# Attention on one core: a head's finishing moved from units 12 to 26 to units 21 to 38 of the next head, projections and latent maxima spread wider

## The reference, cut to what matters

```python
a1 = _attn(q, k1, v1, causal=True)    # keys from a latent
a2 = _attn(q, ks, vs, causal=False)   # 64 selected tokens
a3 = _attn(q, kw, vw, causal=True)    # the "window" keys
out = g[:, 0] * a1 + g[:, 1] * a2 + g[:, 2] * a3
```

## Time and profile before

| | |
|---|---|
| median of three runs | 2782.44 us (2770.95 to 2783.22) |
| the profiled execution | 2779.87 us, its span 2778.1 us |
| PE busy | 2352.7 us, 85% |
| DVE, ACT, POOL busy | 1788.2, 1745.4, 1639.8 us |
| the attention's heads | from 387 us to 2364 us of the span |

### The profile page before, as it was taken

How to read it: one execution, slowest core, us unless ns; L and a number is a source line. 1 busy time by engine, 2 the same in 40 slices (tenths; PEclk the granted TensorE clock), 3 DMA queues, 4 the chain that set the end, 5 groups by cost and what they waited for, 6 DMA issues and landing times. The chain is left out here.

```text
span 2778.1 us, 38402 instructions
## 1 busy us (share of the span) xinstructions
PE 2352.7 (85%) x12402; PEld 1868.3 (67%) x12402; DVE 1788.2 (64%) x2824; ACT 1745.4 (63%) x3574; POOL 1639.8 (59%) x1430
## 2 busy tenths in 40 slices
PE   0278569999999899999999999999999998448885
PEld 0155347777777677777767777777777776448885
DVE  2566357686776768687776868676675763455553
ACT  3433226777777676777767676777777777106663
POOL 5154316767576666767666666766656566006885
PEclk9975559999999999999999999999999999658998
DMA  9757543325051534424151533222132110615776
GB/s 383 320 186 243 167 129 103 86 71 138 20 157 26 132 64 109 97 61 134 40 141 26 138 65 102 56 69 64 24 67 54 31 29 10 186 57 183 193 207 167
DMA packets 199860, 314.87 MB, mean 113 GB/s; under 512 B 95915, under 2 KB 130219, under 8 KB 186731
## 3 DMA queue, kind: packets, MB, share of 16 engines
q1 hardware_dynamic: 189947, 298.23, 37.6%
q0 software_dynamic: 9712, 14.18, 2.7%
HBM read 210.20 MB, written 101.75 MB: 112 GB/s over the span
## 5 line engine op out<-in xcount | busy, mean ns | idle before, releaser
L1391 POOL TENSOR_TENSOR p_lo<-prob,p_hi 128x512 fp32r<-128x512 f32 (+2 forms) x960 | 1096.3, 1151 | 648.0 <-ACT p_hi L1469 513.4
L1467 ACT ACTIVATE prob<-ps_s 128x512 f32<-128x512 f32 (+4 forms) x1344 | 723.3, 538 | 501.0 <-PE ps_s L1484 377.2
L1602 DVE TENSOR_REDUCE max_part<-ps_x 128x1 f32<-128x128 f32 (+1 forms) x1240 | 720.0, 605 | 214.6 <-PE ps_x L1513 131.9
L1469 ACT ACTIVATE p_hi<-ps_s 128x512 fp32r<-128x512 f32 (+3 forms) x1344 | 718.8, 535 | 1.6
L1391 DVE TENSOR_TENSOR p_lo<-prob,p_hi 128x512 fp32r<-128x512 f32 (+1 forms) x320 | 290.3, 907 | 142.3 <-ACT p_hi L1469 133.9
L1570 PE MATMUL ps_o<-p_hi,v_win 128*128 128x512 f32 (+3 forms) x640 | 255.4, 399 | 0.0
L1570 PE MATMUL ps_o<-p_hi,v_lat 128*128 128x512 f32 (+3 forms) x640 | 246.7, 386 | 0.0
L1572 PE MATMUL ps_o<-p_lo,v_win 128*128 128x512 f32 (+3 forms) x640 | 238.5, 373 | 0.0
L1572 PE MATMUL ps_o<-p_lo,v_lat 128*128 128x512 f32 (+3 forms) x640 | 234.5, 367 | 0.0
L1663 DVE TENSOR_TENSOR raw_o<-ps_o,low_sum 32x512 f32<-32x512 f32 x192 | 131.4, 684 | 72.9 <-ACT low_sum L1455 61.4
L1513 PE MATMUL ps_x<-k_hi,head_first 96*128 96x512 f32 (+2 forms) x320 | 123.5, 388 | 42.0 <-DVE max_part L1602 25.5
(11 more groups left out here) (432 smaller groups left out, 5864.5 us busy)
## 6 DMA issues: line engine op xcount, KB each, us to landing
raw<-in_experts_w_dram SPq DMA_DIRECT2D x23, 1536.0 KB
wbuf<-in_tok_weight_dram SPq DMA_DIRECT2D x16, 2000.0 KB, 16.9
head_first<-kw_scratch SPq DMA_DIRECT2D x72, 256.0 KB, 5.0
kw_scratch<-st_hi SPq DMA_DIRECT2D x48, 256.0 KB, 2.9
kw_scratch<-st_lo SPq DMA_DIRECT2D x48, 256.0 KB, 4.4
q_scratch<-st_hi SPq DMA_DIRECT2D x48, 256.0 KB, 3.7
q_scratch<-st_lo SPq DMA_DIRECT2D x48, 256.0 KB, 5.0
head_first<-q_scratch SPq DMA_DIRECT2D x48, 256.0 KB, 6.2
```

The lines of the kernel that those rows point to most:

```text
L1391: ns.tensor_tensor(upper if low else p_lo[:, i % LSLOTS, c:CH], prob[low:P, i % NPROB, c:CH], upper.bitcast(F32), ALU.subtract).then_inc(s ...
L1467: nc.scalar.activation(prob[low:P, i % NPROB, c:CH], ps_s[i % 3][low:P, c:CH], ACT.Exp, scale=SCALE).then_inc(s["p_full"], 1)
L1469: nc.scalar.activation(p_hi[:, i % SLOTS, c:CH], ps_s[i % 3][:, c:CH], ACT.Exp, scale=SCALE).then_inc(s["p_up"], 1)
L1602: ins = nc.vector.tensor_reduce(mpart[:, q, c:c + 1], bank[:, 0:w], axis=AX.X, op=ALU.max)
```

## The change

Three tables move, and three lines of SP's order. No instruction is added or removed.

```diff
         if h + 4 < H:
-            spread(h, prep_tasks(h // 4 + 1, h % 4), *((1, 19) if h else (6, 24)))
-        spread(h, max_tasks(h, LATENT, range(NJ)), 9, HU - 5)
-        spread(h, [("neg", h, 0)], HU - 5, HU - 4)
+            spread(h, prep_tasks(h // 4 + 1, h % 4), *((1, 25) if h else (6, 30)))
+        spread(h, max_tasks(h, LATENT, range(NJ)), 5 if h else 7, HU - 4)
+        spread(h, [("neg", h, 0)], HU - 4, HU - 3)
         if h + 1 < H:
-            spread(h, max_tasks(h + 1, SELECT, None) + max_tasks(h + 1, WINDOW, range(NJ)), HU - 4, NU - 7)
+            spread(h, max_tasks(h + 1, SELECT, None) + max_tasks(h + 1, WINDOW, range(NJ)), HU - 3, NU - 7)
...
-                if h:
-                    store_inverse(h - 1)
-                    load_weight(h - 1)
                 if prep:
                     store_out(gr, j, "kw", 0)
...
                         load_q(h + 1)
                         load_kw(h + 1, 0)
                 if h:
+                    store_inverse(h - 1)
+                    load_weight(h - 1)
                     store_output(h - 1)
...
-        FINISH = {12: 0, 18: 1, 20: 2, 22: 3, 24: 4, 26: 5}
+        FINISH = {21: 0, 30: 1, 32: 2, 34: 3, 36: 4, 38: 5}
```

## The result

| | before | after |
|---|---|---|
| median | 2781.41 us (4 runs, 2770.95 to 2783.22) | 2897.89 us (4 runs, 2888.86 to 2905.29) |
| profiled execution | 2779.87 us | 2888.86 us, span 2887.1 us |

The change is slower: ratio 1.0419, 95% interval 1.0389 to 1.0448, 116 us by the medians. The forecast was +68 and its range ended at +116: the sign was right, the size was not. The median lies 2 us above the range.

The account below looks back on a forecast made before the run. PE, busy for 85% of the span, was taken as the bound, its stalls as what can be won. Terms 16 + 63 - 9 - 2 = +68 us on 2779.9 gave 2848 us, range 2770 to 2896.

Parts of the forecast that it names:

- the eight heads: Heads 1, 2, 4, 5, 6, 8, 9, 10: 127.2 us each, +16 us together, -11 to +44 with all the ends.
- heads 12 to 14: Heads without projections, SP free, weights ahead of step 1: 115.25 us each, -9 us together (-12 to -6).
- head 0: First head, no finishing but six more units for its projections: -2 us (-4 to 0).
- Three heads with loads between: Heads 3, 7 and 11: inverses' store queued behind nine loads, PE stalls 20.2 us, 143.0 us a head: +63 us.
- Chain to the weights: From PE's start of unit 21 through POOL, stores, inverses and weight loads: weights land after 22.9 us, in the eight heads.
- PE stalls for 5.3 us: At unit 33 in the eight heads, PE runs out of `ps_x` banks as DVE awaits weights: 5.3 us, ends 3.5 and 7.2.
- The low clock behind it: Half clock behind the unit 33 stall in the eight heads: 2.5 us a head, between 1.7 and 3.4.
- I leave 1.75 us of stalls per head: Short PE stalls remaining at units 21, 26, 27 and among steps at units 30 to 38: 1.75 us, ends 1.0 and 2.5.
- No wait at step 1: Rival: weights arrive before PE runs out of banks in all eleven heads with projections: 2714 us, chance 0.08.
- Inverses that overtake the loads: Rival: in heads 3, 7 and 11 inverses land before the nine loads, +39 us there: 2814 us, chance 0.10.
- Only three heads wait: Rival: POOL does `st_lo` of kw earlier, so only heads 3, 7 and 11 stall, 15 us: 2770 us, chance 0.08.
- Spreading that does nothing for short stalls: Rival: 1.75 us becomes some 3.5 in 14 heads, +25 us, 2873 us; part of the forecast's chance of 0.74.

Follow-up runs that it names:

- one half: Kernel before with the change's wider tables for projections, maxima and turn; finishing at units 12 to 26 and SP's order stay as before: 2804.73 us, 1.0077.
- the kernel with the later turn: Kernel after with only the turn moved one unit later, to unit 41 instead of 40: 2844.31 us, 1.0239.
- SP's order of before: Kernel after with SP's lines for inverses and weights back ahead of the first kw store, tables as in the change: 2859.85 us, 1.0286.
- the finishing and the queue alone: Kernel before with the change's finishing steps at units 21 to 38 and SP's new order, other tables as before: 2762.5 us, 0.9929.

## Why the prediction was wrong in size

By the table of heads the loss is 40 us above the forecast: 35 in the eight heads and 13 in heads 12 to 14, less 7 in head 0 and 1 in heads 3, 7 and 11.

- **Three heads with loads between** (+63): measured +62. The mechanism is as forecast, the closeness of the number is in part luck: head 3's PE wait is 17.0 us where 20.2 was forecast; the turn and its low clock in head 7 (147.0 us) make up for heads 3 and 11 (141.9 and 139.8), with 143.0 forecast for each.
- **Chain to the weights** (22.9 us after unit 21): 22.6, and PE goes on 23.95 us after unit 21 (24.8). But "PE stalls for 5.3 us" at unit 33 was 2.1 to 2.9 in six of the eight heads, and nothing in heads 4 and 5: PE had lost 2.0 us (3.6 in heads 4 and 5) at units 25, 26 and 28 behind maxima, so the chain had less left to hold up. Sum and end were nearly right, the place was not. "The low clock behind it", 2.5 us, did not come behind unit 33 in heads 1, 2, 6 and 8 (head 1 is the first row of the last section) and came in heads 9 and 10.
- **The step that failed** is "I leave 1.75 us of stalls per head", with its ends 1.0 and 2.5, three or four short ones, some of them "among the steps at units 30 to 38". It priced the steps as work beside maxima, and took it that spreading maxima wider can only help. It did not ask what comes right behind the last maximum: the turn, for which PE needs that maximum read, and ahead of which, in the order written, it can do nothing else. In its place stand, in heads 1 to 11, 1.4 us at unit 13 and 1.8 at units 25 and 26; and at the turn up to 2.3 us of wait, behind 1.8 us or more of which 10 to 14 us at half clock follow (in head 15 they do not), worth 8.5 us in head 12. Moving the last maximum two units away gave 85 us back. Heads 9 and 10, in which the turn cost 0.6 us, came out at 127.4 and 126.1, with 127.2 forecast; that closeness is in part luck, since short stalls above 1.75 us and a wait at unit 33 below 5.3 offset each other.
- **Heads 12 to 14** (-9): +4, the same step. Without the turn they take 111.0, not 115.25: the 113.5 us taken as the cost without stalls was itself read from a head at clock 0.99, and a busy PE at 0.99 still holds low clock.
- **Head 0** (-2): -9 in this profile, 128.4 us. Other kernels here with the same table for its projections (at units 6 to 30) show it at 130.3 to 136.1 us, so a part of the 9 is chance of the one execution.
- **The rivals.** No wait at step 1: wrong. Inverses that overtake the loads: wrong, 9.1 us to land. Only three heads wait: wrong, though in heads 4 and 5 PE does not wait at unit 33. Spreading that does nothing for short stalls, +25, came nearest: it put them at some 3.5 us a head, and units 13, 25 and 26 cost 3.2 in heads 1 to 11 (none in heads 12 to 14). It did not name the turn either. **The range** ended 2 us below the result because its upper end took every known cost at its worst and held no cost from a wait that was not there before.

## What to carry to other kernels

When work is moved on an engine that is not the bound, look in the order of its instructions for the next place where the bounding engine needs one result at once, without a spare buffer, and ask what now stands ahead of it there. Test moved parts together and apart: here one half lost 22 us, the other won 20, and both lost 116, and one wait hid another behind it in three heads. A result that a later step needs belongs in the queue at the point where it is ready, behind what was ready before and ahead of what waits for other things: too early it held the stores, too late the weights.

## What was not expected of the chip

- In these rows the time at low clock behind a wait does not go with the length of the wait. Stretches of the kernel after, behind the waits at unit 33 of head 1 (2.7 us) and head 3 (17.0 us):

```profile
572.80:577.00 4.20, 4.20 (x20) 3.19 (x21) 4.14 (x8) 2.47 (x5) 1.47 (x2) 1.00 0.00 0
852.40:856.00 3.60, 3.59 (x10) 2.79 (x11) 3.54 (x7) 0.88 (x2) 0.17 (x1) 0.50 0.00 0
856.00:862.00 6.00, 6.00 (x24) 4.65 (x23) 5.57 (x7) 4.21 (x8) 3.97 (x3) 0.82 0.00 0
```

Behind 2.7 us it did not fall; behind 17 us, during which it had fallen, it was 0.50 for 3.6 us and back within 6 us more; behind 2.3 us at the turn of head 12 it was 0.50 for 10.9 us. Before, it was 3.4 to 6.8. Short matmuls of 64 columns follow the turn; whether they keep the clock low was not settled, but they do not lower it by themselves, as the kernel with the later turn shows. Head 15, behind whose turn no maxima of a next head stand, short or long, has the same wait of 2.3 us in the kernel after: the clock stays at 1.00 there. With SP's order of before it is low for 6.8 us in head 15 and for 13.7 to 17.1 us in heads 12 to 14. That points at what follows the turn, but not at the short matmuls alone.
- A turn's wait of 2.3 us was followed by half clock in all of heads 12 to 14 of the kernel after, one of 1.3 us in one of these three with the finishing and the queue alone, and one of 1.2 us in none with the later turn. So about 1 us of wait more at the turn went with 5 to 7 us more in a head: heads 12 and 14 take 114.5 us with the finishing and the queue alone, 112.9 with the later turn, and 120 in the kernel after. It is no sharp edge: with SP's order of before, 2.1 us at the turn lowered the clock in heads 2 and 4 and not in heads 5 and 7.
